# A third stage whose four batches are packed into parts of TensorE's array and whose rounds are interleaved

## The reference

```python
# third block: x1 = x, x2 = ctx, per batch 128 x 256
q = einsum('bcn,dc->bnd', x1, Wq) + bq            # d = 16
k = einsum('bcn,dc->bdn', x2, Wk) + bk[:, None]   # d = 16
v = einsum('bcn,dc->bdn', x2, Wv) + bv[:, None]   # d = 128
attn = softmax(einsum('bnd,bdm->bnm', q, k), axis=2)
x = einsum('bcm,bnm->bcn', v, attn) + x1
# fourth block: x and ctx, 64 inner channels
g_x, phi_x, theta_x = (1x1 maps of ctx, ctx, x to 64 channels, each with its bias)
y = theta_x (phi_x g_x) / 256                     # regrouped by associativity
wy = w_w y + w_b
out = gamma * (wy - mean) / sqrt(var + eps) + beta + x
```

## Time and profile before

| | |
|---|---|
| time, median of 3 runs | 1376.34 us (1374.86 to 1376.57) |
| the profiled execution | 1375.4 us, its span 1373.7 us |
| TensorE busy over the span | 1246.0 us (91%) |
| VectorE, ScalarE, GpSimd busy | 942.0, 837.2, 497.7 us |
| stage C in the trace | about 1257.7 to 1370.4 us, then the last store |
| one round of stage C | 25.53 us |

### The profile page before, as it was taken

One profiled execution on the slowest core, in us unless ns is written; L12 is line 12 of the kernel. 1 busy time (PEld: TensorE's weight loads), 2 busy tenths in 40 slices (PEclk: granted clock), 3 DMA queues, 4 the chain that ended last, 5 costly groups with the idle time before them and its releaser, 6 DMA issues. The chain is left out here.

```text
span 1373.7 us, 31155 instructions
## 1 busy us (share of the span) xinstructions
PE 1246.0 (91%) x10866; PEld 1011.5 (74%) x10866; DVE 942.0 (69%) x1843; ACT 837.2 (61%) x2494; POOL 497.7 (36%) x490
## 2 busy tenths in 40 slices
PE   3788999898998749999999999999999999995997
PEld 2667777787787648888888888888888888882554
DVE  2777978879787566666666766666666666662554
ACT  2688877887886545555555555555655556552453
POOL 2455555445544103333333333333333333342000
PEclk9899999999999979999999999999999999997999
DMA  8000000000000020000000000000000000000100
GB/s 312 9 14 20 10 21 8 11 11 16 5 13 1 1 77 1 2 9 1 2 9 0 8 0 0 9 0 0 8 0 9 0 0 1 1 1 26 46 31 31
DMA packets 18547, 24.96 MB, mean 18 GB/s; under 512 B 1360, under 2 KB 16912, under 8 KB 18064
## 3 DMA queue, kind: packets, MB, share of 16 engines
q1 hardware_dynamic: 18448, 23.77, 5.1%
HBM read 21.67 MB, written 2.10 MB: 17 GB/s over the span
## 5 line engine op out<-in xcount | busy, mean ns | idle before, releaser
L1192 POOL TENSOR_TENSOR prob<-prob,l_z_inv 128x512 f32<-128x512 f32 x256 | 261.0, 1040 | 457.1 <-DVE l_z_inv L1433 457.1
L1352 ACT ACTIVATE prob<-psum,l_neg_max 128x256 f32<-128x256 f32 x512 | 235.6, 473 | 245.9 <-DVE l_neg_max L1427 231.9
L741 ACT ACTIVATE ring_e<-ring_e,neg_max 128x128 f32<-128x128 f32 x512 | 164.7, 410 | 15.1 <-DVE neg_max L906 15.0
L1427 DVE TENSOR_REDUCE l_neg_max<-psum 128x2 f32<-128x512 f32 x256 | 164.0, 682 | 10.6 <-PE psum L1246 10.6
L1258 PEld LDWEIGHTS psum<-ident,prob 128*128 128x128 f32 x1024 | 109.8, 141 | 49.0 <-issue 45.4
L1274 PE MATMUL psum<-pT,vs 128*64 128x256 f32 x1024 | 138.8, 391 | 6.7 <-DVE aTl L1443 6.5
L1258 PE MATMUL psum<-ident,prob 128*128 128x128 f32 x1024 | 140.0, 280 | 0.0
L1438 DVE COPY pT<-psum 128x512 f32<-128x512 f32 x128 | 88.2, 689 | 51.1 <-PE psum L1258 51.0
L448 POOL TENSOR_TENSOR ring_e<-ring_e,cross_add 128x512 f32<-128x512 f32 x64 | 83.2, 1308 | 95.2 <-DVE ring_e L901 95.2
L448 POOL TENSOR_TENSOR ring_e<-ring_e,self_add 128x512 f32<-128x512 f32 x64 | 85.4, 1348 | 81.5 <-DVE ring_e L901 80.8
L1443 DVE TENSOR_TENSOR aTl<-psum,aTh 128x256 fp32r<-128x256 f32 x128 | 54.4, 425 | 73.9 <-ACT aTh L1367 73.9
(11 more groups left out here) (197 smaller groups left out, 3226.9 us busy)
## 6 DMA issues: line engine op xcount, KB each, us to landing
wz_raw<-wz_in SPq DMA_DIRECT2D x2, 1536.0 KB, 14.4
x_in<-x SPq DMA_DIRECT2D x8, 256.0 KB, 2.8
cT<-ctxT SPq DMA_DIRECT2D x8, 256.0 KB, 2.9
w<-w_in SPq DMA_DIRECT2D x2, 1024.0 KB, 11.6
l_ub<-ctx_in SPq DMA_DIRECT2D x8, 256.0 KB, 2.7
cg<-ctx_in SPq DMA_DIRECT2D x4, 512.0 KB, 3.7
out<-fin SPq DMA_DIRECT2D x4, 512.0 KB, 2.8
wi_raw<-wi_in SPq DMA_DIRECT2D x1, 1536.0 KB, 17.2
```

What stands on the lines that cost most here:

```text
L741: last = nc.scalar.activation(e, e, ACT.Exp, bias=neg_max[:, n % RE, h:h + 1])
L1192: pool.tensor_tensor(e, e, z_inv[:, t % RE, h, :].unsqueeze(2).broadcast_to([P, 2, D]), ALU.mult)\
L1352: last = nc.scalar.activation(prob[:, t % RE, h, qt * D:(qt + 1) * D], score_bank[h][:, qt * D:(qt + 1) * D], ACT.Exp, bias=neg_max[:, t % ...
L1427: nc.vector.tensor_reduce(neg_max[:, t % RE, h, :], score_bank[h].rearrange("p (t c) -> p t c", t=2), AX.X, ALU.max, negate=True).then_inc ...
```

## The change

Only stage C, the layout of its weights and the bias columns are changed.

- **Packing.** Queries and keys of the four batches go to four quarters of the output partitions (32 each, 16 of them zero weights), into one bank; ScalarE reads each with one instruction of 128 partitions into `qk`. Scores contract over 32 partitions, each batch in its own quarter of rows and its own bank (`score_bank`, now four). Theta and phi g go to halves of the output partitions, the products with `ww` and the last matmuls use halves of the rows. `x` is read from `xs` without the copy.
- **Division.** GpSimd multiplies the probabilities (`norm`); VectorE only takes the reciprocal (`inverse_sums`). GpSimd also adds the last bias to `x2` (`bias`, into `x2b`), and VectorE makes the output with one operation for two batches (`output`).
- **Order.** The loops are written out. The next round's queries, keys, values and scores stand inside the present round, theta after them, and the last matmuls of a round stand in the next one. The transposes write over the scores' banks. `cg`, `x2`, `x2b` and `fin` are double.
- **SyncE.** The load of round i + 2 stands behind the store of round i. TensorE waits for all six weight transfers at the start.

```diff
-        names = ["q0", "q1", "k0", "k1"] + [f"w{b}" for b in range(G)] + ["g", "h", "t0", "t1", "y0", "y1"]
-        work = Banks(ctx, nc, "l2_work", names, [psum[:, 6 + j, :] for j in range(2)])
+        score_bank = [psum[:, b, :] for b in range(G)]
+        wide = Banks(ctx, nc, "l2_wide", ["p0", "p1", "p2", "p3", "y0", "y1"], [psum[:, 4 + j, :] for j in range(2)])
+        work = Banks(ctx, nc, "l2_work", ["qk", "w0", "w1", "w2", "w3", "t", "g", "h"],
+                     [psum[:, 6 + j, :] for j in range(2)])
...
+            load(1)
+            for i in range(ROUNDS):
+                store(i)
+                if i + 2 < ROUNDS:
+                    sp.wait_ge(*work.full("w3", i))
+                    load(i + 2)
...
+            def norm(i, b):
+                pool.wait_ge(*z_inv_done.at(i, b))
+                e = prob[:, b, :].rearrange("p (t c) -> p t c", t=2)
+                pool.tensor_tensor(e, e, z_inv[:, b, :].unsqueeze(2).broadcast_to([P, 2, D]), ALU.mult)\
+                    .then_inc(probs_done.sem, 1)
...
+            def queries_keys(i):
+                ps = work.psum("qk")
+                pe.wait_ge(*work.free("qk", i))
+                pe.wait_ge(*ctx_in[i % 2].at(i // 2))
+                for t in range(2):
+                    for b in range(G):
+                        src = xs[:, i * G + b, :] if t == 0 else cg[i % 2][:, b, :]
+                        last = mm(ps[quarter(b), t * D:(t + 1) * D], wqk[:, t, :], src, start=True, stop=True)
+                last.then_inc(work.fills("qk"), 1)
+
+            def scores(i):
+                pe.wait_ge(*work.out("qk", i))
+                for b in range(G):
+                    pe.wait_ge(*probsT_done.at(i - 1, b))
+                for qt in range(2):
+                    for b in range(G):
+                        last = mm(score_bank[b][:, qt * D:(qt + 1) * D], qk[quarter(b), 0, qt * P:(qt + 1) * P],
+                                  qk[quarter(b), 1, :], start=True, stop=True)
...
+            def heads(i):
+                ps = work.psum("h")
+                pe.wait_ge(*work.free("h", i))
+                pe.wait_ge(*work.out("g", i))
                 for m in range(2):
...
+                    for b in (2 * m, 2 * m + 1):
+                        last = mm(ps[half(b), m * P:(m + 1) * P], gT[half(b), m, :], ww[half(b), :],
                                   start=True, stop=True)
...
+            for i in range(ROUNDS):
+                more = i + 1 < ROUNDS
+                gram(i)
+                if i > 0:
+                    last_maps(i - 1)
+                turn(i, 0)
+                turn(i, 1)
+                heads(i)
+                times_v(i, 0)
+                turn(i, 2)
+                if more:
+                    queries_keys(i + 1)
+                times_v(i, 1)
+                turn(i, 3)
+                times_v(i, 2)
+                if more:
+                    values(i + 1, 0)
+                times_v(i, 3)
+                if more:
+                    scores(i + 1)
+                    for b in range(1, G):
+                        values(i + 1, b)
+                thetas(i)
+            last_maps(ROUNDS - 1)
...
+            read_queries_keys(0)
+            for i in range(ROUNDS):
+                exponentials(i, 0)
+                exponentials(i, 1)
+                if i > 0:
+                    read_thetas(i - 1)
+                exponentials(i, 2)
+                read_gram(i)
+                exponentials(i, 3)
+                turned_out(i, 0)
+                turned_out(i, 1)
+                read_heads(i)
+                turned_out(i, 2)
+                if i + 1 < ROUNDS:
+                    read_queries_keys(i + 1)
+                turned_out(i, 3)
+            read_thetas(ROUNDS - 1)
...
+            for i in range(ROUNDS):
+                maxima(i, 0)
+                maxima(i, 1)
+                inverse_sums(i, 0)
+                maxima(i, 2)
+                inverse_sums(i, 1)
+                maxima(i, 3)
+                if i > 0:
+                    for b in range(1, G):
+                        read_values(i, b)
+                inverse_sums(i, 2)
+                inverse_sums(i, 3)
+                if i > 0:
+                    output(i - 1, 0)
+                    output(i - 1, 1)
+                add_x(i, 0)
+                add_x(i, 1)
+                add_x(i, 2)
+                if i + 1 < ROUNDS:
+                    read_values(i + 1, 0)
+                add_x(i, 3)
```

More of the change, by code:

```diff
@@ L1587, in layers23 @@
+        qk = sb("l2_qk", [P, 2, D])
         vpg = sb("vpg", [P, G, 2, D])
[L1588 to L1599, removed]
@@ L1619, in layers23 @@
+        out_written = [event(f"out{k}_written", 1, 16) for k in range(2)]
         weights_in = sem("l2_weights_in")
[L1620 removed]
         bn_step = sem("bn_step")
[L1623 to L1624 removed]
         block = ctx.enter_context(nc.Block())
@@ new lines, in values, with gram @@
+            def values(i, b):
+                ps = work.psum(f"w{b}")
+                pe.wait_ge(*work.free(f"w{b}", i))
+                for j in range(2):
+                    last = mm(ps[:, j * D:(j + 1) * D], cg[i % 2][:, b, j * P:(j + 1) * P], wvpg[:, :],
+                              start=True, stop=True)
+                last.then_inc(work.fills(f"w{b}"), counts(f"w{b}", i))
+            def gram(i):
+                ps = work.psum("g")
+                pe.wait_ge(*work.free("g", i))
+                pe.wait_ge(*work.out("w3", i))
+                for m in range(2):
+                    for j in range(2):
+                        for b in (2 * m, 2 * m + 1):
+                            last = mm(ps[half(b), m * CI:(m + 1) * CI], vpg[:, b, j, P + CI:D], vpg[:, b, j, P:P + CI],
+                                      start=j == 0, stop=j == 1)
+                last.then_inc(work.fills("g"), 1)
@@ L1756, in _, with last_maps @@
+            def last_maps(i):
                 pe.wait_ge(*work.out("h", i))
+                pe.wait_ge(*work.out("t", i + 1))
+                for h in range(2):
+                    pe.wait_ge(*wide.free(f"y{h}", i))
                 for m in range(2):
-                    pe.wait_ge(*work.out(f"t{m}", i))
-                    ps = bank(f"y{m}", i)
                     for b in (2 * m, 2 * m + 1):
-                        last = mm(ps[:, b % 2 * D:(b % 2 + 1) * D], hw[:, b, :], theta[:, b, :],
+                        last = mm(wide.psum(f"y{b % 2}")[:, m * D:(m + 1) * D], hw[half(b), m, :], theta[half(b), m, :],
@@ L1762, in _ @@
                                   start=True, stop=True)
-                    last.then_inc(work.fills(f"y{m}"), 1)
+                        if m == 1:
+                            last.then_inc(wide.fills(f"y{b % 2}"), 1)
+            pe.wait_ge(weights_in, 96)
+            queries_keys(0)
+            for b in range(G):
+                values(0, b)
+            scores(0)
+            for i in range(ROUNDS):
[21 more added lines that the diff above has]
+                thetas(i)
```

359 lines of the change are left out of this document (161 added, 198 removed).

## The result

The changed kernel takes 1363.35 us (median of five runs, 1359.28 to 1364.72), the kernel before 1376.22 beside it (1374.86 to 1376.57): a ratio of 0.9906, 95% interval 0.989 to 0.9922, so 12.9 us less. Forecast were 1366, 1357 to 1375. The profiled execution of the changed kernel is the fastest of the five, 1359.28, with a span of 1357.6.

A forecast was written before the change was run, and what follows sets the result against it. TensorE time bounds the third stage first (busy 92% of a round), covered waits second. Start and rounds summed to 1355.3; 5.0 after the stage, 5.1 for clock falls and 0.94 to the median gave 1366 us, range 1357 to 1375.

The forecast's parts named there:

- three falls of the clock: Stage C: three of six TensorE gaps bring half clock, delaying TensorE 1.7 us each, 5.1 us in all.
- wait for VectorE: Rounds 1 to 3: fourth batch's values wait for VectorE's read of `w1` behind the fourth maxima, 2.4 us idle.
- wait for the context: Rounds 1 and 2: next queries wait for a context load issued behind the store, TensorE idle 3.2 us.
- Phi g stays 1.15: Phi g burst in each round: stays 1.15 us because the number of weight loads is unchanged.
- The `ww` products: Products with `ww` in each round: stay at the unpacked 1.16 us; at half, the whole would be 1.1 shorter.
- 17.4 us of work a round: TensorE in a stage C round: burst durations laid end to end give 17.4 us in place of 23.4.
- rival (e): Changes of matmul shape: 0.33 us idle each on top of the bursts, 3.0 us in round 0; 1374 us, chance 0.05.
- 0.2 us a round longer each: Queries, keys and scores: by the skill's 3.07 times packing speedup, each would be 0.2 us a round longer.
- (c): Stage C packed matmuls don't overlap: 33 us over the stage, so 1399 us; chance 0.05.
- (d): Rounds 1 to 3: the two waits don't bite, as `w1` reads or the store come earlier; 1348 us, chance 0.05.
- (a): Stage C gaps: none or one fall of the clock, 1361.3 to 1363 us; chance 0.18.
- (b): Stage C: five or six clock falls, or a load of 4.5 plus the store's whole transfer; 1375 us, chance 0.17.

The follow-up runs named there:

- experiment 3: Changed kernel with the context load ahead of the store and the values of batches 1 and 2 read between the maxima: 1343.29 us.
- experiment 6: Changed kernel with each score matmul contracting over all 128 rows, so scores no longer work side by side: 1364.56 us.
- Experiment 8: Changed kernel with VectorE multiplying the probabilities behind each reciprocal again, instead of GpSimd: 1371.18 us.
- experiment 1: Changed kernel with the next context load placed ahead of the store of the round before: 1351.22 us.
- experiment 4: Changed kernel with packed scores issued batch by batch instead of a quarter of each in turn: 1360.46 us, one run.
- experiment 9: Changed kernel with the queries of rounds 2 and 3 computed nine times ahead of the context wait, keeping TensorE busy: 1359.24 us.
- experiment 7: Changed kernel with load ahead of store, values read between maxima, and scores contracted over all 128 rows: 1349.41 us.
- experiment 10: Changed kernel with load ahead of store, values read between maxima, and first queries waiting only for their own weights and context: 1340.74 us.

## Why the prediction was right, and where it wasn't

The forecast's mechanism held: both new waits at the places named, three falls of the clock, rounds of the right order. That the time came within 3 us was partly luck, as the sum was 6.1 us too high. Position by position in the profiled execution, with forecast and measured times:

| step | forecast | measured |
|---|---|---|
| first scores end | 1273.1 | 1272.67 |
| round 0 (without a fall) | 14.8 | 14.03, of it 0.9 a fall |
| rounds 1, 2 (without) | 22.9 | 23.91, 23.78, of it 1.6 a fall |
| wait for VectorE | 2.4 | 2.21, 2.21, 2.20 |
| wait for the context | 3.2 | 4.46, 4.33 |
| round 3 | 21.6 | 19.74 |
| falls | 3 x 1.7 | 0.9 + 1.6 + 1.6 |
| VectorE's last end, with three falls | 1360.4 | 1354.13 |

The 6.3 us between the two last ends are 0.4 at the start, 1.7, 0.6, 0.7 and 1.9 in rounds 0 to 3 without their falls, and 1.0 in the falls. Two mis-sized terms, the next two paragraphs, explain most of it.

**Packing.** Queries and keys follow each other to the next burst in 1.00 (forecast 1.07), scores in 1.08 (1.17), theta 1.08 and last maps 1.14 (1.08) with their tails: right. Two terms were too large. "Phi g stays 1.15, since its bound is the loads of weights" was wrong: with the loads in column halves, 16 take 0.58 us where they took 1.01, and the burst 0.69. The `ww` products, forecast at the unpacked 1.16, take 0.65. Together that is 1.0 us a round of TensorE's work too much; for the half of it the forecast had named the price itself, "at half of it the whole would be 1.1 shorter".

**Bursts laid end to end with their tails.** This is the larger mis-sized term. TensorE was to have 17.4 us of work a round, and at full clock it has 15.2; of these 2.2, packing explains 1.0. Behind the context landing the forecast had 7.0 us of work to the scores' end. In experiment 3, at full clock, the same bursts start one behind the other at intervals of 1.00, 0.97, 0.44, 0.86, 0.87, 0.95 and 1.08, together 6.17. A burst's duration holds a tail that the next one overlaps: transposes of 0.60 hold TensorE 0.44. With phi g and `ww` it explains most of the 1.9 us by which round 3 was forecast too long, and of the 1.7 in round 0.

**The drain.** In the trace of after, at full clock, the weight loads stand idle for 0.33 us, in some places 0.17, at the changes of shape where nothing else is waited for, and not between bursts of 128 by 128. The Trainium skill's "Mode switching requires drain" (TensorEngine Tiling, Key Properties) agrees with that, but the start-to-start intervals above already contain it: rival (e) adds it a second time and is refuted, since the rounds are shorter, not longer. As a ratio, the gain of the packed scores is 3.15 in experiment 6 (3.62 / 1.15), where the column quarters gave 3.7. The Trainium skill's 3.07 times (TensorE: Matmul & The Clock Gate, Measured speedup vs the span model) is near that. As a time my row was the nearer one all the same: it gave 1.17 for a burst that took 1.15, while the unpacked 3.91 divided by the Trainium skill's 3.07 is 1.27, an estimate. The forecast's "0.2 us a round longer each" is that estimate against the queries' 1.07; against the scores' 1.17 it is 0.1.

**The load.** It was issued 11.0 us after the scores' end (forecast 11.65), since TensorE and VectorE were early, and landed 4.9 and 4.8 us later in rounds 1 and 2, more than the forecast's 4.3 and its "4.5 at worst". That both errors cancel at the landing, 16.0 against 15.95 for the queries' start, is luck. The wait is longer than forecast because TensorE had less work in front of it, not because the context came late; where a transfer sets the time, less work of TensorE's in front of it only means a longer wait.

**Division and bias.** GpSimd divides two batches in 2.04 us (forecast 1.04 each). The bias, 0.92 each, hides behind the chain as forecast. Experiment 8 prices the move at 7.8 us, falls of the clock included, a gain that the forecast held only implicitly.

**The falls.** Three out of six, as forecast, at 1275.6, 1302.9 and 1326.8: both context waits and the wait for the first division. The three waits for VectorE, 2.2 each, had none here; in experiments 1, 4 and 9 some did. Which wait brings one was a guess. Over stage C of the eleven traces with the packing it can be counted: the clock fell in or behind each of the ten context waits of 4.2 to 4.9 us, the three waits of 3.42 for VectorE in experiment 8 and the twelve waits of 2.1 to 2.7 for a division, behind five of the twelve waits of 2.2 for VectorE's reads, and behind none of the six of 1.1 to 1.4. So for the waits of 2.2 it stays a guess. Their price was near: from the queries' start to the next transposes are 3.61 us in the trace of after (1302.73 to 1306.34) and 1.97 in experiment 3 (1299.00 to 1300.97), so 1.6; from the first transposes to the first product 3.09 in round 0 and 2.17 in experiment 7, which had the full clock there, so 0.9. A fall can cost more: in round 0 of experiment 3 the clock stayed low for 6.8 us, from 1277.2 to 1284.0, twice as long as here.

**From the profiled execution to the median.** Its 1359.28 are 6.1 below the forecast's 1365.4 (the stage 6.3 shorter, 0.2 more behind it). The median is 4.07 above it, where the forecast took 0.94 as for the kernel before. So the forecast missed the median by only 2.65 because a sum 6.1 too high met a spread 3.1 larger than assumed: that is luck. What makes the other executions longer is in no trace of this kernel. Two things that vary were seen in others: the untouched stages before ended up to 3.5 us later (the last group of the stage before starts at 1254.97 here and at 1258.49 in experiment 1), and round 0 took 14.2 (experiment 10) or 16.1 us (experiment 3) with the clock low in less or more of it. Their shares stay open.

**Rivals.** (c), packing that doesn't overlap, is refuted; its price too: undoing the scores' share, priced at 11, cost 1.2 to 5.0 in experiment 6 and 6.1 in experiment 7. It took every burst as critical. (d) is refuted, and experiment 3 shows what it would have been: 1343, where its price was 1348 (its terms add up to 1341.7 before the ends, not 1342.3). (a) and (b) differ from the forecast in the number of falls, and the trace has three. The median alone couldn't have told (a) from the forecast: 1363.35 is nearer to (a)'s 1363 than to 1366.

## What to carry to other kernels

When a change takes work off the bounding engine, list for every in-order queue what now stands ahead of the thing that the engine will ask for next. Here a read behind four maxima and a load behind a store gave back all or most of what the interleaving had hidden, and moving two pieces of code brought 20 us more. Price bursts from start to start, not by durations laid end to end, and price the undoing of a part by the engine that a round is short of: the same 2.5 us of TensorE cost 1.0 to 1.2 a round beside a wait and 2.06 without one.

## What the runs showed of the hardware

- Weight loads of 64 columns in alternate column halves overlap like the matmuls: 16 in 0.55 to 0.58 us against 1.01.
- Products over two halves of the rows that write into the two halves of one PSUM bank's partitions overlap: the eight `ww` records took 0.65 us against 1.16 in the kernel before, all in one half of the rows (their weights have 64 columns now in place of 128), hardly more than four records of the same 128 columns in the transposes, 0.60.
- The order in which the packed scores are issued made no difference (1.15 and 1.17 us for 16 records, one run).
- The first of four batches' results of a burst of 3.62 us was read 2.36 after the burst's start, of one of 1.15 us 1.16 after.
- A context load of 512 KB issued 0.4 us behind a store of the same size landed after 4.9 and 4.8 us in the changed kernel, and after 4.6 to 6.1 us in the eighteen such cases of the eleven traces; the 26 loads there with no store just ahead took 3.8 to 4.4, and those inside the rounds of the kernel before 3.5 to 3.8.
- In stage C a wait of TensorE of 3.4 us or more always had the lower clock in or behind it (13 of 13), one of 2.1 to 2.7 for a division too (12 of 12), one of 2.2 for VectorE's reads in five cases of twelve, one of 1.1 to 1.4 in none of six.
